# A graph kernel's attention loop: twenty-four batches in the loop body in place of six

## The reference

```python
h = x @ Wr; s = h @ a_src; d = h @ a_dst
e = leaky_relu(s[src] + d[dst]); e = where(mask, e, -inf)
m = segment_max(e, dst); w = where(mask, exp(e - m[dst]), 0)
alpha = w / segment_sum(w, dst)[dst]
out = out + segment_sum(alpha[:, None] * h[src], dst) + br      # for each r of 8
```

## Time and profile before

| | us |
|---|---|
| median of 3 runs | 3840.04 (3839.91 to 3840.69) |
| span of the profiled execution | 3833.0 |
| around the span, by the median | 7.0 |
| attention's turns in the profile | from about 205 to 1739 |

### The profile page before, as it was taken

One profiled execution on the slowest core, in us unless ns is written; L12 is line 12 of the kernel. 1 busy time (PEld: TensorE's weight loads), 2 busy tenths in 40 slices (PEclk: granted clock), 3 DMA queues, 4 the chain that ended last, 5 costly groups with the idle time before them and its releaser, 6 DMA issues. The chain is left out here.

```text
span 3833.0 us, 77662 instructions
## 1 busy us (share of the span) xinstructions
PE 2849.0 (74%) x16134; PEld 1989.3 (52%) x16135; DVE 2312.7 (60%) x8562; ACT 1473.1 (38%) x3352; POOL 2309.6 (60%) x1835
## 2 busy tenths in 40 slices
PE   7277777777777776565889897878887787877863
PEld 4155555555555554342344365656666565656651
DVE  7299989989999997685242254343444434343433
ACT  1055555555555554341000043433433333333431
POOL 0277666766676666430000048888888888888882
PEclk7565655656555665567989979988888999898986
DMA  4544434444443445884332335555555555555544
GB/s 135 100 112 114 125 106 111 123 109 111 125 112 109 119 115 94 85 162 117 107 105 78 111 40 55 53 55 53 54 54 53 55 53 55 52 54 53 53 46 91
DMA packets 661597, 336.51 MB, mean 88 GB/s; under 512 B 436912, under 2 KB 625123, under 8 KB 660580
## 3 DMA queue, kind: packets, MB, share of 16 engines
q0 software_dynamic: 148736, 86.57, 23.6%
q1 hardware_dynamic: 447430, 110.13, 14.0%
q10 hardware_dynamic: 65248, 138.05, 9.7%
HBM read 156.42 MB, written 202.84 MB: 94 GB/s over the span
## 5 line engine op out<-in xcount | busy, mean ns | idle before, releaser
L2181 POOL DMA_INDIRECT sums<-el_rows,el_idx x816 | 1269.2, 1555 | 611.8 <-DVE el_rows L2395 363.5
L820 POOL DMA_INDIRECT at_hs<-table,at_rec_s x976 | 1032.7, 1058 | 506.9 <-PE near_ps L961 301.6
L858 ACT CAST at_count_s<-near_ps 128x400 f16<-128x400 f32 x976 | 482.5, 494 | 686.7 <-PE near_ps L961 624.3
L961 PE MATMUL near_ps<-at_pair_hot,at_src_low_hot 128*128 128x425 f16 x976 | 486.2, 498 | 349.4 <-ACT at_count_s L858 268.2
L2393 DVE CAST el_idx<-el_place 128x4 uint32<-128x4 f32 x204 | 35.3, 173 | 837.5 <-DMA sums<-el_rows,el_idx 806.2
L933 PEld LDWEIGHTS sums_ps<-at_hw,at_hit 128*128 128x128 f32 x1952 | 461.5, 331 | 20.7 <-issue 14.8
L933 PE MATMUL sums_ps<-at_hw,at_hit 128*128 128x66 f32 x1952 | 441.7, 408 | 8.3 <-DVE acc L1007 8.3
L961 PEld LDWEIGHTS near_ps<-at_pair_hot,at_src_low_hot 128*128 128x128 f16 x976 | 134.5, 138 | 507.3 <-ACT at_count_s L858 348.5
L2329 ACT ACTIVATE el_h<-el_h_ps,el_valid 128x128 f32<-128x128 f32 x816 | 232.6, 368 | 248.1 <-PE el_h_ps L2243 248.1
L999 DVE TENSOR_SCALAR at_pair_hot<-iota_wide,at_rec_s 128x400 f16<-128x400 f16 x976 | 322.0, 332 | 2.4
L2197 PE MATMUL el_miss_t<-ident_b,el_miss 128*128 128x128 bf16 x816 | 84.7, 266 | 290.6 <-DVE el_miss L2367 290.6
(11 more groups left out here) (374 smaller groups left out, 4973.7 us busy)
## 6 DMA issues: line engine op xcount, KB each, us to landing
slots<-at_count_s ACTq DMA_DIRECT2D x122, 850.0 KB
el_rec<-attr SPq DMA_DIRECT2D x816, 32.0 KB
chunk<-slots SPq DMA_DIRECT2D x256, 100.0 KB
attr<-in_edge_attr SPq DMA_DIRECT2D x19, 1248.0 KB
chunk<-slots ACTq DMA_DIRECT2D x208, 100.0 KB
at_rec_s<-meta SPq DMA_DIRECT2D x992, 3.5 KB
at_hs<-table,at_rec_s POOLq DMA_INDIRECT x976
el_pair<-meta SPq DMA_DIRECT2D x816, 1.0 KB
```

Source lines behind the costliest of these rows:

```text
L820: pool.indirect_dma_start(hs[:, s, u, :], None, k.table, bass.IndirectOffsetOnAxis(rec[:, s, u, 0:1].bitcast(U32), 0)).then_inc(gathered[s ...
L858: a.copy(count[:, (n.o + d) % 2, i, 0:AW], near[:, (n.o + d) % 2, 0:AW]).then_inc(count_ready, 1)
L961: pe.matmul(near[:, s, 0:SW], low_hot[:, s, i, :], pair_hot[:, s, i, :], start=False, stop=True, skip_group_check=(i > 0)).then_inc(near_r ...
L2181: pool.indirect_dma_start(k.sums_flat[a], bass.IndirectOffsetOnAxis(idx[:, j, a:a + 1], 0), rows[:, j, a, :], None, compute_op=ALU.add).th ...
```

## The change

The loop's body holds `LONG = 24` turns in place of 6, on every engine. The loop takes `WHOLE = (122 - 6) // 24 = 4` passes, turns 6 to 101. Turns 102 to 123 stand behind it, written out one by one, 22 in place of 4. Buffers stay as they are: `RING` is still six deep.

Two things follow in SP's stream. A part of the attribute copy is still issued every six turns within the loop, but there are 4 x 4 = 16 such parts in place of 19, so the last copy, behind the clears, holds 20352 rows in place of 5376. And the turns behind the loop leave out loads past batch 121, which the loop's body could not: the two loads for batches 122 and 123 go.

```diff
+LONG = 4 * RING
+WHOLE = (NB0 - RING) // LONG
-        return self.o * per + more if self.it is None else self.it * (RING * per) + (self.o * per + more)
+        return self.o * per + more if self.it is None else self.it * (LONG * per) + (self.o * per + more)
...
     for o in range(first, RING):
         step(Turn(o))
-    whole = NB0 // RING - 1
-    with eng.Fori(0, whole) as it:
-        for o in range(RING):
+    with eng.Fori(0, WHOLE) as it:
+        for o in range(LONG):
             step(Turn(RING + o, it))
-    for o in range(RING * (whole + 1), NB0 + 2):
+    for o in range(RING + LONG * WHOLE, NB0 + 2):
         step(Turn(o))
...
-        PARTS = NB0 // RING - 1
+        A_LOOP = LONG // RING
+        PARTS = WHOLE * A_LOOP
...
-                if n.it is not None and n.o == RING:
-                    records(n.it, CR)
+                if n.it is not None and n.o % RING == 0:
+                    records(n.it * A_LOOP + (n.o // RING - 1), CR)
```

More of the change, by code:

```diff
@@ L58 @@
 assert NB0 * B <= NV and NB3 * B <= NV and NG < GW
-assert NB0 % RING == 2 and 2 * P * B <= 2048 and NB0 <= P
+assert RING + LONG * WHOLE + 4 <= NB0 and 2 * P * B <= 2048 and NB0 <= P
 class Steps:
@@ L659, in __call__ @@
     def __call__(self, per, more=0):
-        return self.o * per + more if self.it is None else self.it * (RING * per) + (self.o * per + more)
+        return self.o * per + more if self.it is None else self.it * (LONG * per) + (self.o * per + more)
     def round(self, d):
         r = (self.o + d) // RING
-        return r if self.it is None else self.it + r
+        return r if self.it is None else self.it * (LONG // RING) + r
     def pairs(self, d):
         r = (self.o + d) // 2
-        return r if self.it is None else self.it * (RING // 2) + r
+        return r if self.it is None else self.it * (LONG // 2) + r
     def has(self, d):
@@ L772, in load, with records @@
                     sp.dma_start(rec[:, s, u, :], k.meta[bass.ds(offs[u], P), :]).then_inc(rec_loaded[s], 16)
-            def records(it, rows):
+            def records(part, rows):
                 to = nc.values_load_multi_w_load_instructions(
@@ L778, in records @@
                     skip_runtime_bounds_check_because="0 or EP + P")[1][0]
-                sp.dma_start(k.attr[bass.ds(to + it * CR, rows), :].rearrange("(p r) f -> p (r f)", p=P),
-                             k.edge_attr[bass.ds(it * CR, rows), :].rearrange("(p r) f -> p (r f)", p=P)
+                sp.dma_start(k.attr[bass.ds(to + part * CR, rows), :].rearrange("(p r) f -> p (r f)", p=P),
+                             k.edge_attr[bass.ds(part * CR, rows), :].rearrange("(p r) f -> p (r f)", p=P)
                              ).then_inc(rec_written, 16)
```

## The result

The changed kernel takes 3781.57 us (median of 4 runs, 3779.75 to 3782.62), the kernel before 3839.97 (4 runs, 3835.15 to 3840.69) on the same chip: a ratio of 0.9854 [0.984, 0.9868], or 58.4 us less. The forecast was 3780, its range 3760 to 3802. The profiled execution took 3782.62 with a span of 3780.9, so 1.7 us lie around the span, not 7.0. Runs of before show 2.0 to 2.1 as well: the profiled execution of before, with its span of 3833.0, must then have taken about 3835, a quick one among runs near 3840.

A forecast was written before the change was run, and what follows sets the result against it. DVE was taken to bound the attention's loop, losing time at its jumps back, and the DMA engines the filler. Terms -53.0 - 1.5 + 4.5 - 10 + 0 = -60 took the span from 3833.0 to 3773, so 3780 us; range 3760 to 3802.

The forecast's parts named there:

- term A: Attention loop before the filler: 13 of DVE's 16 jumps back go, at 4.08 us each, -53.0 us.
- Register work (B): Turns 102 to 107: straight code works out no wait counts in registers, 0.3 us a turn, -1.5 us.
- The other engines' stalls (C): Three remaining jumps: longer bodies make other engines fetch too, mostly within DVE's hole; +4.5 us, bounds 0 and 12.3.
- The rival's 3799: First rival's upper case at the three jumps: PE's fetch twice DVE's, ACT's behind it; chance 0.16 for 3788 to 3800.
- The filler (D): Filler stretch at the attention's end: two jumps and up to 27.4 us of issue waits go, -10 us credited.
- at 90% in place of 83% a batch takes 16.0 us: Filler: a higher DMA engine share shortens batches from 17.4 us; 12 batches save 17 us, of which 10 taken.
- my second rival: Filler eats its gain: DVE's issue waits become waits for stores and gathers, 3790 us; chance 0.14.
- SP's end (E): End of SP's stream: earlier clears, three copy parts behind them, covered by 17 us; 0, or +10 if cover is gone.
- 7.0 us around the span: Time outside the profiled span, taken from the runs' median of 3840.04; added to span 3773 to give 3780.

The follow-up runs named there:

- the second profiles: The kernel before and the changed kernel, each profiled once more with nothing changed: 3842.12 and 3780.22 us.

## Why the prediction was right

**The hole is DVE's, and it goes with the jump (term A): right.** Forecast -53.0; the issue waits at `at_top` fell from 65.2 to 12.5, -52.7. DVE alone gives the whole gain, the other engines alone nothing. That the hole is a fetch the prediction took for granted; the code packets in the traces bear it out. In the kernel before, DVE's branch ends at 411.19 us. Queue q14, one of the two instruction queues of the earlier trace rows, moves no packet from 411.3 to 414.1 us, then this one (the queue from 414.1 to 414.6 us), and DVE goes on at 416.01:

```profile
q14 instruction: 1, 0.01, 3.9%
```

Each of the 16 holes has just one such packet of 8 KB. It starts 0.95 to 3.01 us behind the branch, and DVE goes on 1.15 to 1.53 us after its end. At the first of the two jumps in the filler it starts only 9.2 us behind the branch; that is the wait of 10.9 us in the earlier trace rows. Straight code is fetched too, but ahead, beside the work. In the kernel without a loop on DVE, from 350 to 1350 us:

```profile
q14 instruction: 38, 0.31, 0.1%
```

The Trainium skill ("Runtime: NRT & Kernel Launch", section "Instruction fetch mechanics") says that fetching ahead follows the code in sequence, and that a taken branch to code that is not held has to wait for a fetch; both halves agree with the runs, 3.8 to 5.0 us behind DVE's jumps and no hole in 1110 us of straight code.

**Register work (B): near in size, but not from the row that it was read from.** Turns 102 to 106 take 55.5 us in place of 57.7, so 2.2 us less in five turns; forecast -1.5. The 17 waits at `at_key` come once a pass, not once a turn, so 0.3 us a turn was a misreading, and that the size came out near is luck. The straight version's 0.21 us a turn over 90 turns may be of the same kind.

**The other engines' stalls (C): the mechanism was right, the price was not.** All four stall at their three jumps, PE for 3.3 to 3.5 us. I charged +4.5. The holes of DVE are no longer with them than without (12.5 and 12.1 us), and turns 12 to 102 take 1048.2 and 1048.0 us: nothing. The lower bound was the answer: at the jump at 544 us PE comes back two microseconds before DVE, and ACT at the same moment. (The rival's 3799 counts 8 us a jump in all; "8 more each" on top of 3788 would have been 3812.)

**The filler (D): the term that was mis-sized.** Forecast -10. From turn 102 to the end of the last `acc` 298.5 us became 294.3; without B that is 4.2 - 2.2 = 2.0 us of gain (3.2 in the second profiles). The step that failed is "at 90% in place of 83% a batch takes 16.0 us". The DMA share did rise, to 65.6 + 12.2 + 10.0 = 88%, but the gathers' own share stayed (65.1, now 65.6), and with it their pace: 85 gathers in 187 us, 17.6 us a batch, before 17.4. The rise went to q1, 5.47 MB in place of 2.14, where the clears had come in. They did not eat the gain: with 24 turns on DVE alone the clears begin at 1599 us and not at 1573, and the part from turn 102 takes 292.9 us, hardly less. The gathers were held by their one row, 695 ns a packet, as spreading the rows showed. On this term my second rival was right: DVE's 27.4 us of issue waits became waits for sums and stores. That its time of 3790 did not come is mainly because C had been charged too much.

**SP's end (E): right, at nothing.** The clears ran in the filler stretch and the barrier (views of the two lines) shows SP first, against the earlier trace rows:

```profile
L798 SPq DMA_DIRECT2D sums<-zero x32: 435/800/8623, 1573.3 to 1633.6; - x32
```

```profile
L699 SPq COMPARE_BRANCH  x1: 43/43/43, 1663.6 to 1663.6; - x1
L699 DVEq COMPARE_BRANCH  x1: 47/47/47, 1679.9 to 1679.9; - x1
```

SP has 16.3 us of cover, before 17.1; the earlier start of the clears added none. A single clear took up to 8.6 us to issue, and it did not matter.

**The sum.** The forecast's -60 stands beside -59.3 at the end of the attention: A -52.7, B -2.2, C about 0, D -2.0, another -1.2 from before the first turn, and -1.2 that I cannot place. That the sum is so near is in part luck, since C was 4.5 too dear and D 8.0 too generous. A second pair also cancelled: I counted 7.0 us around the span where there are 1.7, and the part behind the attention came out 7.1 longer in the profiled execution; in the kernel before it differs by 5.4 between two executions.

## What to carry to other kernels

Look at what the engine that sets the pace does at a loop's jump back: a hole with nothing waited for, at every jump and of much the same length (here 2.7 to 4.8 us), is a price per jump, and here a longer body of that engine alone took it away, while the others kept their short loops. Count how many such holes the profile has outside of stretches with another limit, and in those stretches ask what holds the other limit before crediting a gain (here one row that all filler gathers read, worth 51 us by itself). With both, and straight code on DVE, this kernel goes from 3839.8 to 3689.46 us.

## What the hardware showed that I had not expected

- Which bodies stall at the jump, by the instructions that the trace records in one pass, the sequencer's included: DVE's 474, and at twelve turns ACT's 394, SP's 351 and POOL's 314 to 319 do; ACT's 199, SP's 177 and POOL's 158 to 163 at six turns do not. PE's 1242 at twelve turns do not, its 2478 at twenty-four do. I had expected stalls only from bodies about as long as DVE's.
- PE, ACT and DVE fetching at about the same time do not slow each other noticeably: DVE's three holes last 12.5 us together with the others' and 12.1 alone.
- Gathers that all read one row take 695 ns a packet, spread ones 85 to 94, and transfers of other queues are late beside the slow ones: ACT's waits for its stores add up to 73.9 us in the filler of the changed kernel, and to 6.0 with the rows spread.
- A forward branch of PE that is taken once took 0.45 us in one execution and 2.69 us in another of the same program.
